# Attention and pooling on one core: score matmuls of two heads issued together, the residual kept on chip, four smaller moves

## The reference

```
q = (side + b_self) @ Wq + bq                      # 16 heads of 16
k = concat(x + b_prev, side + b_self) @ Wk + bk
v = concat(x, side) @ Wv + bv
score = q . k[x part] / 4, keys beyond the batch's length set to -inf
self  = sum(q * k[side part]) / 4                  # one more score per position and head
w     = softmax(concat(score, self))
x     = x + (w[:-1] @ v[x part] + w[-1] * v[side part]) @ Wo + bo
# pooling
z = tanh(x @ W1 + b1) @ v1                          # one score per position
p = softmax over l of z, masked to l<=j, l>=j or l!=j by the batch's kind
x = x + (p @ x) / count(mask)
```

## Time and profile before

| what | value |
|---|---|
| three runs | 326.65, 340.59, 363.67 us (median 340.59) |
| span of the profiled execution | 364.1 us; its own time is not listed apart, the nearest run is 363.67 |
| PE busy / PEld / DVE / ACT / POOL | 328.1 / 253.8 / 192.8 / 168.1 / 75.9 us |
| mean granted TensorE clock | 0.787 of 2.4 GHz |
| DMA | 35.52 MB, 98 GB/s in the mean |

### The profile page before, as it was taken

One profiled execution on the slowest core, in us unless ns is written; L12 is line 12 of the kernel. 1 busy time (PEld: TensorE's weight loads), 2 busy tenths in 40 slices (PEclk: granted clock), 3 DMA queues, 4 the chain that ended last, 5 costly groups with the idle time before them and its releaser, 6 DMA issues.

```text
span 364.1 us, 6371 instructions
## 1 busy us (share of the span) xinstructions
PE 328.1 (90%) x2100; PEld 253.8 (70%) x2100; DVE 192.8 (53%) x446; ACT 168.1 (46%) x361; POOL 75.9 (21%) x87
## 2 busy tenths in 40 slices
PE   3968999899999999999999999999999878987543
PEld 2956786776777787787878877787887646664522
DVE  3585444314253337767576776657676655323331
ACT  5321214533233435576566556666656644256030
POOL 6150110021020301152034114213411400320310
PEclk9995555555555559999999999999999965569866
DMA  5295257020810204920863393076329101000000
GB/s 146 75 310 130 86 151 171 3 86 30 234 30 4 86 2 130 213 99 31 217 136 118 104 227 109 29 196 155 115 80 198 44 3 31 31 31 0 32 0 29
DMA packets 28023, 35.52 MB, mean 98 GB/s; under 512 B 4440, under 2 KB 24416, under 8 KB 28000
## 3 DMA queue, kind: packets, MB, share of 16 engines
q1 hardware_dynamic: 27360, 33.12, 34.4%
q0 software_dynamic: 640, 2.10, 1.6%
HBM read 20.26 MB, written 14.69 MB: 96 GB/s over the span
## 4 chain that ended last, share of the span: by engine, by line
PE 84%; DVE 6%; issue 3%; DMA 3%; ACT 2%; SPq 0%; POOL 0%; DVEq 0%; ACTq 0%
PE ps_any L1000 27%; PE ps_max L1026 17%; PE ps_any L1051 11%; PE ps_exp L1038 9%; PE ps_any L1007 7%; PE ps_any L1215 4%; PE ps_any L1111 2%; PE ps_any L1151 2%; PE ps_any L1083 2%; PE ps_any L1060 2%; DMA k_rows<-k_spill 1%; DVE s_max L801 1%; DMA w_raw<-in_L_cond_Wq 1%; DMA k_spill<-k_lo 1%; PE ps_max L1072 1%
## 5 line engine op out<-in xcount | busy, mean ns | idle before, releaser
L801 DVE TENSOR_REDUCE s_max<-ps_max 128x2 f32<-128x512 f32 x128 | 87.4, 688 | 84.2 <-PE ps_max L1026 84.1
L530 ACT ACTIVATE pt<-ps_exp 128x512 f32<-128x512 f32 x128 | 75.6, 598 | 83.5 <-PE ps_exp L1038 82.5
L1026 PE MATMUL ps_max<-k_rows,q_rows 49*128 49x256 f32 x256 | 73.4, 394 | 4.9 <-DVE s_max L801 2.8
L1026 PEld LDWEIGHTS ps_max<-k_rows,q_rows 49*128 49x128 f32 x256 | 44.9, 232 | 30.5 <-issue 19.8
L1038 PE MATMUL ps_exp<-q_rows,k_rows 51*128 51x256 f32 x256 | 57.8, 328 | 0.3 <-ACT pt L530 0.2
L1038 PEld LDWEIGHTS ps_exp<-q_rows,k_rows 51*128 51x128 f32 x256 | 45.7, 232 | 3.2 <-ACT pt L530 1.9
L1051 PE MATMUL ps_any<-pt,v_aug 128*32 128x256 f32 x512 | 42.2, 456 | 1.8 <-ACT pt L530 1.8
L488 POOL TENSOR_TENSOR attn<-num,rden 128x256 f32<-128x256 f32 x16 | 9.6, 623 | 88.0 <-DVE rden L941 88.0
L1051 PEld LDWEIGHTS ps_any<-pt,v_aug 128*32 128x32 f32 x512 | 15.0, 123 | 15.6 <-issue 8.2
L1000 PE MATMUL ps_any<-st_hi,w_hi 128*128 128x256 f32 x64 | 23.3, 364 | 1.0 <-DVE st_lo L828 1.0
L477 POOL TENSOR_TENSOR prod_lo<-prod,prod_hi 128x512 fp32r<-128x512 f32 x8 | 10.2, 1281 | 65.3 <-ACT prod_hi L626 65.3
(11 more groups left out here) (143 smaller groups left out, 650.9 us busy)
## 6 DMA issues: line engine op xcount, KB each, us to landing
q_rows<-q_spill SPq DMA_DIRECT2D x32, 192.0 KB, 4.3
k_rows<-k_spill SPq DMA_DIRECT2D x32, 192.0 KB
q_spill<-q_hi SPq DMA_DIRECT2D x16, 256.0 KB, 2.5
k_spill<-k_hi SPq DMA_DIRECT2D x16, 256.0 KB, 2.5
s_sb<-in_fside_BxSxS SPq DMA_DIRECT2D x8, 256.0 KB, 5.1
x_sb<-in_x SPq DMA_DIRECT2D x8, 256.0 KB, 4.3
q_spill<-q_lo SPq DMA_DIRECT2D x8, 256.0 KB, 2.1
k_spill<-k_lo SPq DMA_DIRECT2D x8, 256.0 KB, 3.2
```

Of the source, the lines that this page charges most:

```text
L530: nc.scalar.activation(pt[:, h % 8], ps_exp[:, h % 2], ACT.Exp).then_inc(p_ready, 1)
L801: nc.vector.tensor_reduce(s_max[:, h // MG, :, h % 2, h // 2 % MJ], ps_max[:, h % 2], AX.X, ALU.max).then_inc(max_found, 1)
L1026: last = pe.matmul(ps_max[:, e, t], q_rows[par][rows, j, P * t:P * t + P], k_rows[par][rows, j, :], start=True, stop=True)
```

## The change

- **Heads in pairs.** Slots become 16 steps; in every even step TensorE issues four matmuls for two heads at once, alternating between rows 0.. and rows 64.. (`pair_for_max`, `pair_for_exp`), into both halves of `ps_max` or `ps_exp`. DVE reduces the pair in one instruction over 1024 elements, ACT takes its exponential in one. TensorE may score pair j when DVE (ACT) is done with pair j-1. The output columns of q and k are grouped so that a product's half m holds pairs 4m to 4m+3.
- **Maxima.** The two transposes of a group of maxima become one of 32 columns; `mt_sb` holds 32 x 128, and `place_max` issues four DMAs for two.
- **Residual.** x_bo (x plus bias) is made one period ahead from `x_sb`, four batches deep; the DMA of L375 goes. Loads move to the top of SP's period; the k spill stands ahead of `place_max` of group 0, and the spill buffers in DRAM are doubled.
- **Pooling.** One tensor_tensor_reduce per half adds the mask and takes the maximum. GpSimd builds `hidden`.
- **High parts on GpSimd.** GpSimd copies q_hi from q_full (but for batch 0) and x1_hi from x1, ahead of its subtractions. The product q*k is no longer split: four float32 matmuls with `headsum` take the place of eight.
- **v_wide and z_sb** are padded with zeros to 128 rows.
- **Start.** Wq and the bias vectors are loaded from ACT's queue, ahead of `weight_hi(0)`: eleven DMAs, eight of them for bq and bk (before: two). `split_bias_inputs` stands ahead of `weight_lo(0)` on DVE; `setup_v` comes later.
- **No loop.** All eleven periods are written out.

```diff
-            def score_for_max(i, k, h):
-                par, e, j = k % 2, h % 2, h // 2
-                if (n := count(i, k, H, h - 1)) is not None:
-                    pe.wait_ge(max_found, n)
-                rows = slice(64 * e, 64 * e + KM)
-                for t in range(KB):
-                    last = pe.matmul(ps_max[:, e, t], q_rows[par][rows, j, P * t:P * t + P],
-                                     k_rows[par][rows, j, :], start=True, stop=True)
+            def pair_for_max(b, j):
+                par = b % 2
+                if (n := count(b, PAIRS, j)) is not None:
+                    pe.wait_ge(max_found, n)
+                for half in range(KB):
+                    for e in range(2):
+                        rows = slice(64 * e, 64 * e + KM)
+                        last = pe.matmul(ps_max[:, e, half], q_rows[par][rows, j, P * half:P * half + P],
+                                         k_rows[par][rows, j, :], start=True, stop=True)
...
+            def max_of(b, j):
+                dve.wait_ge(max_scored, count(b, PAIRS, j + 1))
+                nc.vector.tensor_reduce(s_max[:, j // MJ, :, :, j % MJ].rearrange("p t e -> p e t"),
+                                        ps_max[:], AX.X, ALU.max).then_inc(max_found, 1)
...
+                nc.scalar.activation(pt[:, j % 4].rearrange("p e t s -> p (e t s)"),
+                                     ps_exp[:].rearrange("p e t s -> p (e t s)"), ACT.Exp).then_inc(p_ready, 1)
...
+                pe.transpose(bank[0:KB * 4 * MJ, 0, 0:P], neg_max[:, g].rearrange("p t e c j -> p (t e c j)"),
+                             ident[:]).then_inc(mt_ready, 1)
...
                 for e in range(2):
+                    for t in range(KB):
+                        at = 4 * MJ * t + 2 * MJ * e
+                        sp.dma_start(q_rows[b % 2][64 * e + R_MAX:64 * e + R_MAX + 2, MJ * g:MJ * g + MJ,
+                                                   P * t:P * t + P].bitcast(F32),
+                                     mt_sb[at:at + 2 * MJ, g, :]).then_inc(max_placed[g], 16)
...
+                    if nxt > 0:
+                        nc.gpsimd.tensor_copy(q_hi[:], q_full[:]).then_inc(q_hi_done, 1)
+                    nc.gpsimd.tensor_tensor(q_lo[:], q_full[:], q_hi[:].bitcast(F32), ALU.subtract
...
+                    nc.gpsimd.tensor_scalar(hidden[:], side_of[:], code[:, old:old + 1],
+                                            MASKED, ALU.is_equal, ALU.mult).then_inc(hidden_done, 1)
...
+                    nc.gpsimd.tensor_copy(x1_hi[:], x1[:]).then_inc(x1_hi_done, 1)
...
+                    nc.gpsimd.tensor_tensor(x_bo[:, nxt % 4], x_sb[:, nxt % 2],
...
+                            nc.vector.tensor_tensor_reduce(
+                                out=masked[:, half], in0=ps_any[:, bank_free("SB", t)[0], 0], in1=hidden[:, half],
+                                scale=-1.0, scalar=3e38, op0=ALU.add, op1=ALU.min,
+                                accum_out=row_max[:, half:half + 1]).then_inc(masked_done, 1)
...
+            act.dma_start(w_raw[:, 0], Wq.rearrange("(k p) n -> p k n", p=P)).then_inc(weights_loaded[0], 16)
+                for n, vec in enumerate((bq, bk)):
+                    for e in range(2):
+                        for g in range(NM):
+                            act.dma_start(bqk_raw[64 * e:64 * e + 64, n, g:g + 1],
+                                          vec.rearrange("(g j e d) -> g e d j", g=NM, e=2, d=DH)[g, e].unsqueeze(2)
+                                          ).then_inc(bias_loaded, 16)
```

More of the change, by code:

```diff
@@ L300, in load @@
                         sp.wait_ge(st_ready, n)
[L301 to L314, removed]
@@ L505, in _ @@
[L505 to L511 removed]
+                            attn[:, half].rearrange("p (h d) -> p h d", d=DH),
+                            num[:, half].rearrange("p (h d) -> p h d", d=DH),
+                            rden[:, half].unsqueeze(2).broadcast_to([P, H, DH]), ALU.mult).then_inc(attn_done, 1)
@@ L512, in _ @@
+                if live(old):
+                    pool.wait_ge(out_done, count(old, 1, 1))
+                    pool.dma_start(out_rows[old], o_out[:]).then_inc(out_stored, 16)
+            for t in PERIODS:
+                period(t)
             pool.wait_ge(out_stored, 16 * B)
@@ L702, in _ @@
+            weight_hi(0)
+            for t in PERIODS:
+                period(t)
         @block.vector
@@ new lines, in pair_for_exp @@
+            def pair_for_exp(b, j):
+                par = b % 2
+                if j % MJ == 0:
+                    pe.wait_ge(max_placed[j // MJ], count(b, 64, 64))
+                if (n := count(b, PAIRS, j)) is not None:
+                    pe.wait_ge(p_ready, n)
+                for half in range(KB):
+                    for e in range(2):
+                        rows = slice(64 * e, 64 * e + KF)
+                        last = pe.matmul(ps_exp[:, e, half], k_rows[par][rows, j, P * half:P * half + P],
+                                         q_rows[par][rows, j, :], start=True, stop=True)
@@ L1077, in self_scores @@
             def self_scores(bank):
-                by_block = bank[:, 0, 0:2 * H].rearrange("p (g t e j) -> p t e g j", g=NM, t=KB, e=2)
-                for t in range(KB):
-                    for e in range(2):
-                        for part in (prod_hi, prod_lo):
-                            last = pe.matmul(by_block[:, t, e], part[:, e, P * t:P * t + P], headsum[:],
-                                             start=(part is prod_hi), stop=(part is prod_lo))
+                for g in range(NM):
+                    for half in range(KB):
+                        at = 8 * (KB * g + half)
+                        last = pe.matmul(bank[:, 0, at:at + 8], prod[:, g, P * half:P * half + P],
+                                         headsum[:].rearrange("p e j -> p (e j)"), start=True, stop=True)
                 return last
@@ L1150, in period @@
-                            for j, (kb, w, x) in enumerate(terms):
-                                last = pe.matmul(bank[0:A, 0], w[:, kb, :], x[:, kb, :],
+                            bank = take_bank("Z", t)
+                            pe.wait_ge(x1t_hi_done, count(old, 1, 1))
+                            pe.wait_ge(x1t_lo_done, count(old, 1, 1))
+                            pe.wait_ge(w1_lo_done, 1)
+                            terms = [(kb, w, part) for kb in range(KB)
+                                     for w, part in ((w1_hi, x1t_hi), (w1_lo, x1t_hi), (w1_hi, x1t_lo))]
@@ L1152, in period @@
+                            for j, (kb, w, part) in enumerate(terms):
+                                last = pe.matmul(bank[0:A, 0], w[:, kb, :], part[:, kb, :],
                                                  start=(j == 0), stop=(j == len(terms) - 1))
```

921 lines of the change are left out of this document (408 added, 513 removed).

## The result

The changed kernel takes **393.91 us** (median of 4 runs, 393.34 to 399.80) against 333.62 us before (4 runs, 326.35 to 363.67). That is 1.18 times as long by the medians; the runs before differ by how long TensorE's clock stood low in each, so the comparison goes by the fast runs of both, 393.70 against 326.50 us: 1.206 times as long, 95% interval 1.202 to 1.209. The forecast was 299 us in a range of 276 to 328, faster. It was wrong in sign.

What follows compares the result with a forecast made beforehand. TensorE, at a speed set by its clock, was taken to bound periods 1 to 7. Start and period terms summed to 315 us against the 364.1 us profile, scaled to the median run as 299 us, range 276 to 328.

Steps and rivals of the forecast that it cites:

- New waits: TensorE waiting for reductions and maxima: 2.6 us per period, with no DMA chain behind, k read back 8.0 us early.
- The clock stays low: Rival: TensorE's clock stays at 1.2 GHz or falls back each time it rises, 391 us; chance 0.07.
- Pairing: Score steps on TensorE: two heads overlap, 16 steps become 8, -6.9 us per full period at 2.4 GHz, -11.6 at 1.2.
- The smaller edits: On TensorE: fewer headsum matmuls, v_wide padding and one transpose for two, together 1.0 us saved per period (low clock 1.6).
- Full period: Periods 3 to 6: 24.4 us of TensorE work plus 2.6 of waits, 27.0 us each; bounds 24.4 and 30.
- The maxima's DMAs: Four small DMAs on SP's queue: about 5 us to the last landing, 1 us late per period, or 0 to 3.
- VectorE 19.4 us: DVE's work in a full period falls from 22.9 by 3.5 to 19.4 us, through larger reductions, fused pooling and hidden leaving.
- GpSimd 9.3 us: GpSimd gains two copies and hidden, loses prod_lo: 9.3 us of work in a period of 27, at no cost.
- Start +4 us: Before period 0: bias DMAs on ACT's queue delay the first Q to 13 us; +4 us, bounds 0 and +6.
- The last two periods: Periods 8 and 9 at the end: 21.5 - 3 = 18.5 us and 26.1 - 0.9 = 25.2 us.
- VectorE and the chains become the bound: Rival: DVE keeps most of its waits, so a full period takes 30 us and the kernel 317; chance 0.18.
- The pairs don't overlap: Rival: a paired score step costs 1.33 us, saving only 3.1 + 1.0 us per period; about 325 us; chance 0.03.

Runs made afterwards that it cites:

- e1: Changed kernel with the source of the place DMAs walked with the 16 feature rows outermost instead of the 3 parts: 296.65 us.
- e8: e1 with the pair's matmuls split again, the upper row half's head in the even step and the lower's in the odd one: 370.37 us.
- e10: e1 with bias DMAs issued by SyncE behind Wk, split_bias_inputs after weight_lo(1), and hidden back on VectorE at step 6: 291.64 us.
- e4: Changed kernel with the 16-way read-back for group 0 alone, group 1 (heads 8 to 15) left at the count of 3: 344.39 us.
- e2: Kernel before with the place DMAs' source written with the 3 parts as their own outermost dimension, no padding: 349.39 us against 351.49.
- e3: Kernel before with the 3 parts as outermost source dimension and each spill part padded from 128 to 136 rows: 434.36 us against 341.24.
- e9: e1 with both key blocks of one head ahead of both of the other, instead of alternating row halves: 295.81 us.

## Why the prediction was wrong

**The step that failed** is in "New waits": "but no DMA chain: k is read back from 209.54 on, 8.0 us before period 5 needs it". That took the read-back to last as long as before, without saying so or giving a reason; it does move the same bytes in as many DMAs. The issues and the slack of 8.0 us before the next batch needs the data were read from the right rows. What was not asked is what the new source pattern does to the transfer, though the diff rewrites it. Each edited DMA has a duration of its own to be argued, like an edited matmul. From the first issue of the read-back to the first maxima it is 8.1 us with sixteen engines (e1) and 15.3 with three, and TensorE stood idle for the last 7.35 of them: the slack was gone. No rival had this mechanism. "The clock stays low" gave 391 us, close to the time measured by luck, and the clock did fall back each time it rose; but e1 shows that as a consequence: with the read-back mended it stood at full speed from 64.5 to 238.6 us with all the rest of the change in place.

**With that step mended the rest of the sum can be read off**, in e1:

- Total: 299 forecast, 296.65 measured, which is 9% below the fastest run before. The agreement is partly luck: the clock rose for its long stretch at 64.5 us, earlier than the sum had it (137, less about one period), and the start and the full periods were longer.
- Pairing, -6.9 us a full period at 2.4 GHz: 6.2 measured by undoing it (e8), up to 1.4 of them waits. At 1.2 GHz (-11.6) no run shows it: the lowest clock of a period from 1 to 6 in e1 is 0.87. The smaller edits (-1.0) were not tested one by one.
- Full period 27.0 us: 27.8. TensorE's 24.4 us of work and 2.6 of waits can't be compared singly, as its records run through short waits (26.77 busy). The maxima's DMAs, put 1 us late in every period, made TensorE wait 1.6 us in the whole execution.
- VectorE 19.4 us: 20.1. The reduction of 128x1024 took 1.22 as extrapolated; the fused masking and maximum 0.418 + 0.084 us, against 0.42.
- GpSimd 9.3 us: 10.2. Its copies took 0.60 each, not 0.8, but `hidden` takes 2.01 there. The 1.54 read for it on VectorE was mostly a wait for GpSimd; by itself it takes 0.48. At no cost, as forecast (e10).
- Start +4 us: the first Q product came at 13.37 us against 13 forecast, period 0 at 34.7 against 33.5.
- The last two periods, 18.5 and 25.2: 18.8 and 23.6.
- "VectorE and the chains become the bound" did not come: 27.8 us, not 30. "The pairs don't overlap" fell with e8.

## What to carry to other kernels

When a diff rewrites the access pattern of a DMA, write down both sides' dimensions after merging what is evenly spaced, and look at the slowest one: here 3 in place of 48 turned a gain of 9% (e1 against the fastest run before) into a loss of 21%, with no byte more. In a profile it shows as a DMA line at a few tenths while a transfer is being waited for; compare the rate of that stretch with the same transfer in the kernel before. The number of small packets on the page tells the count before any time does. And a slow transfer that is not due yet is not free: the small DMAs issued after it were late too (e4), and issuing them from another engine's queue brought 5 us of the 48.

## What had not been expected of the hardware

- A read-back of eight DMAs of 192 KB ran at about 75 GB/s with a slowest dimension of 3 (18.9% of sixteen engines) and at 220 with 16 (100%); two DMAs of 8 had 45%. By the packet counts each DMA had one small packet for each engine. While the slow one was under way, a store and loads issued later were moved at up to 371 GB/s between 232 and 236 us.
- Two parts 128 rows apart with 128 rows each are one dimension (e2, no change); with eight rows of padding they are not (e3, +93 us).
- Four score matmuls on two row halves start in twos in either program order (e9), 0.22 us between the twos.
- `hidden`, a tensor_scalar of 128x512, took 2.01 us on GpSimd. On VectorE it took 0.48 us, or 1.24 to 1.54 where a GpSimd instruction had begun just before it; it then ended about 0.28 us after that one. A cast of 128x512 on GpSimd took 0.60 us, and its subtraction of two inputs 1.28.
